# A fused attention and expert kernel: query parts loaded in three transfers in place of six, row maxima in one in place of four

## What is computed

```python
x = x + jnp.tanh(g_xattn[0]) * _L0_xattn_ref(_layernorm(x, axis=-1), ctx_1024, mask_BxSxS2_bf0, ...)
x = x + jnp.tanh(g_ffn[0]) * _L0_ffn_ref(_layernorm(x, axis=-1), ...)
x = x + jnp.tanh(g_xattn[1]) * _L1_xattn_ref(ctx_1024, ctx_1024, _layernorm(x, axis=-1), mask_BxS2_if0, ...)
x = x + jnp.tanh(g_ffn[1]) * _L1_ffn_ref(_layernorm(x, axis=-1), ...)
```

```python
q = heads(tgt @ Wq + bq) / jnp.sqrt(jnp.asarray(D_K, tgt.dtype))
k = heads(memory @ Wk + bk)
scores = jnp.einsum('bhqd,bhkd->bhqk', q, k)
scores = jnp.where(mask[:, None, :, :], NEG_INF, scores)
attn = jax.nn.softmax(scores, axis=-1)
```

## Time and profile before

| | |
|---|---|
| median of three runs | 831.93 us (830.88 to 833.39) |
| the profiled execution | 831.65 us, of which its span is 829.6 us |
| TensorE busy, matmuls | 594.7 us, 72% |
| VectorE busy | 487.7 us, 59% |
| ScalarE busy | 244.0 us, 29% |
| loads of query parts | 24 of 128 KB |
| loads of maxima | 16 of 12 KB |

### The profile page before, as it was taken

How to read it: one execution, slowest core, us unless ns; L and a number is a source line. 1 busy time by engine, 2 the same in 40 slices (tenths; PEclk the granted TensorE clock), 3 DMA queues, 4 the chain that set the end, 5 groups by cost and what they waited for, 6 DMA issues and landing times.

```text
span 829.6 us, 14684 instructions
## 1 busy us (share of the span) xinstructions
PE 594.7 (72%) x6038; PEld 418.9 (50%) x6038; DVE 487.7 (59%) x1173; ACT 244.0 (29%) x421; POOL 42.7 (5%) x52
## 2 busy tenths in 40 slices
PE   2256575968998699777777597988759998406563
PEld 1223122635376478653264486854428887405452
DVE  5736664544136635589446545687255475597765
ACT  0001352304555233204434232315335332201110
POOL 1700000000001100000002000000000000000000
PEclk9977696989999889799998897999979999757655
DMA  3390100210000268710000379300002684058440
GB/s 92 62 305 12 50 2 0 50 20 13 1 1 1 50 160 239 214 53 6 0 21 1 72 252 259 132 5 1 13 0 70 207 231 140 1 142 262 111 143 13
DMA packets 40354, 70.71 MB, mean 85 GB/s; under 512 B 9824, under 2 KB 26577, under 8 KB 40097
## 3 DMA queue, kind: packets, MB, share of 16 engines
q1 hardware_dynamic: 30796, 63.64, 27.6%
q10 hardware_dynamic: 9492, 6.14, 2.6%
HBM read 65.82 MB, written 3.95 MB: 84 GB/s over the span
## 4 chain that ended last, share of the span: by engine, by line
PE 49%; DVE 27%; DMA 9%; issue 6%; ACT 5%; SPq 2%; POOL 1%; POOLq 0%; DVEq 0%; ACTq 0%
PE DOWN L750 12%; PE UP L913 9%; PE RING L949 5%; PE RING L954 3%; DMA OHA<-scratch_positions 3%; DVE nmax L1240 3%; PE MISC L715 2%; PE RING L821 2%; DVE xn L1025 2%; PE MISC L724 2%; DMA OHA<-scratch_q_parts 2%; DVE OHA L1054 2%; DMA QAf<-scratch_q_parts 2%; DVE dots L1379 1%; DVE GV L1441 1%
## 5 line engine op out<-in xcount | busy, mean ns | idle before, releaser
L750 PEld LDWEIGHTS DOWN<-W,hT 128*128 128x128 f32 x1152 | 154.1, 197 | 21.9 <-issue 2.6
L750 PE MATMUL DOWN<-W,hT 128*128 128x128 f32 x1152 | 154.8, 280 | 0.2 <-ACT hT L661 0.2
L661 ACT ACTIVATE hT<-UP,b 128x512 f32<-128x512 f32 x144 | 98.3, 687 | 158.9 <-PE UP L913 158.5
L913 PE MATMUL UP<-xnTf,W 128*128 128x512 f16 x432 | 124.3, 403 | 3.4 <-ACT hT L661 3.0
L949 PE MATMUL RING<-TAB,OHA 128*128 128x32 f16 x2560 | 78.8, 180 | 53.6 <-DVE OHA L1054 32.4
L949 PEld LDWEIGHTS RING<-TAB,OHA 128*128 128x128 f16 x2560 | 74.4, 99 | 61.6 <-DVE OHA L1054 39.0
L688 ACT ACTIVATE GV<-RING 128x256 f32<-128x256 f32 x80 | 30.7, 383 | 149.9 <-PE RING L954 149.9
L1070 DVE SCALAR_TENSOR_TENSOR acc<-DOWN,W,acc 128x128 f32<-128x128 f32 x128 | 36.0, 344 | 59.6 <-PE DOWN L750 53.1
L1054 DVE TENSOR_SCALAR OHA<-OHA,cst 128x2048 f16<-128x2048 bf16 x80 | 59.5, 748 | 13.4 <-DMA OHA<-scratch_positions 12.7
L1240 DVE TENSOR_REDUCE nmax<-RING 128x3 f32<-128x462 f32 (+1 forms) x96 | 53.7, 585 | 19.2 <-PE RING L824 15.1
L913 PEld LDWEIGHTS UP<-xnTf,W 128*128 128x128 f16 x432 | 42.4, 103 | 35.2 <-issue 9.5
(11 more groups left out here) (321 smaller groups left out, 774.2 us busy)
## 6 DMA issues: line engine op xcount, KB each, us to landing
OHA<-scratch_positions SPq DMA_DIRECT2D x80, 512.0 KB, 5.6
OHA<-scratch_tail_positions SPq DMA_DIRECT2D x48, 160.0 KB, 4.9
OHA<-scratch_positions SPq DMA_DIRECT2D x16, 160.0 KB, 3.9
QAf<-scratch_q_parts SPq DMA_DIRECT2D x18, 128.0 KB
hT<-in_w ACTq DMA_DIRECT2D x3, 768.0 KB, 6.1
W<-in_w ACTq DMA_DIRECT2D x3, 768.0 KB
scratch_q_parts<-qs SPq DMA_DIRECT2D x4, 384.0 KB, 2.5
X<-in_x ACTq DMA_DIRECT2D x4, 256.0 KB, 4.9
```

Source lines behind the costliest of these rows:

```text
L661: act.activation(hT[:, i % HS, :], UP[:, i % 2, :], ACT.Silu, bias=b1[:, e, c:c + 1], scale=1.0 / W1SCALE).then_inc(h_ready, 1)
L750: last = pe.matmul(DOWN[:, n % 2, t * 128:(t + 1) * 128], hT[:, (k + c) % HS, t * 128:(t + 1) * 128], W2[:, e, c, :], start=(c == 0), stop ...
L913: last = pe.matmul(UP[:, i % 2, :], W1[:, pw, e, c * 128:(c + 1) * 128], xnTf[:, b % 2, px], start=(n == 0), stop=(n == 2))
```

## The change

The slots are renumbered, so that query parts 0, 1, 2 stand in slots 0 to 2, parts 0, 1 in slots 3 and 4, and part 0 in slot 5; the key parts are paired with them as before. The source rows of a run of slots are then one after the other in `scratch_q_parts`, and each of the three runs in `RUNS` is one load: 24, 16 and 8 partitions, with 16 KB on each. The maxima come back in one load of 3 partitions with 16 KB on each. The waits on `qa_in` and `qm_in` count three loads and one.

```diff
-SLOT_Q = (0, 0, 0, 1, 1, 2)
-SLOT_K = (0, 1, 2, 0, 1, 0)
+SLOT_Q = (0, 1, 2, 0, 1, 0)
+SLOT_K = (0, 0, 0, 1, 1, 2)
+RUNS = ((0, 3), (3, 2), (5, 1))
...
-                    for i, s in enumerate(SLOT_Q):
-                        sp.dma_start(QAs[b][i * DK:(i + 1) * DK], dq[b, s].rearrange("(d h) q -> d h q", d=DK)).then_inc(qa_in, 16)
+                    for at, n in RUNS:
+                        sp.dma_start(QAs[b][at * DK:(at + n) * DK].rearrange("p h q -> p (h q)"),
+                                     dq[b, 0:n].rearrange("s (d h) q -> (s d) (h q)", d=DK)).then_inc(qa_in, 16)
                     if b == 0:
-                        sp.wait_ge(qa_in, 16 * len(SLOT_Q))
+                        sp.wait_ge(qa_in, 16 * len(RUNS))
...
-                    for f in range(4):
-                        sp.dma_start(QAs[b][QR:QM, 4 * f:4 * f + 4].rearrange("s h q -> s (h q)"),
-                                     dm[b, :, 4 * f * NT:4 * (f + 1) * NT].rearrange("s e q -> s (e q)")).then_inc(qm_in, 16)
+                    sp.dma_start(QAs[b][QR:QM].rearrange("s h q -> s (h q)"),
+                                 dm[b].rearrange("s e q -> s (e q)")).then_inc(qm_in, 16)
...
-                act.wait_ge(qa_in, 16 * len(SLOT_Q))
+                act.wait_ge(qa_in, 16 * len(RUNS))
...
-                        pe.wait_ge(qa_in, 16 * len(SLOT_Q) * (b + 1))
+                        pe.wait_ge(qa_in, 16 * len(RUNS) * (b + 1))
...
-                        pe.wait_ge(qm_in, 16 * NT * (b + 1))
+                        pe.wait_ge(qm_in, 16 * (b + 1))
```

## The result

The change makes the kernel 0.8% faster: 825.37 us median (821.84 to 829.56, 20 runs) against 832.09 (828.48 to 835.09, 20 runs of the kernel before beside it), ratio 0.9915 with an interval of 0.990 to 0.993. That is 5.8 to 8.3 us where 14.2 were forecast, and the median lies outside the range of 812.5 to 823.6. The direction held; about half of the gain did not come. The profiled execution of after took 829.56 us (span 827.5), at the upper end of its runs, so a second trace of the same kernel (825.95 us) is read beside it.

A forecast was written before the change was run, and what follows sets the result against it. The prediction took the query loads, limited at their destination partitions, to hold up TensorE in batches 0 and 1. 6.2 + 1.5 + 5.8 + 1.0 - 0.3 = 14.2 us gave 817.7 us, range 812.5 to 823.6.

The forecast's parts named there:

- The set, 6.2 us earlier in batch 0: Query loads: three loads following one another take 6.3 us for 12.5, so the set lands 6.2 us earlier; bounds 5.3 to 8.2.
- What follows in batch 0: Issues behind the set move with it, WvT landing at about 50.4 for 56.6; VectorE's maxima hardly move; 6.2 us passed on.
- Clock in batch 0: After the shorter idling before the first table, part of 56.6 to 68.0 runs at the upper clock: 1.5 us, bounds 0 to 4.3.
- the prediction's last sign of being wrong: The upper clock level after the shorter waits is lost again at another place; no size given.
- Batch 1, the whole wait of 5.8: Before batch 1's score matmuls: the set lands at about 169.0, TensorE is free at 169.4, so 5.8 us of wait go.
- Clock in batch 1: Score stage of batch 1, entered without a pause, falls from 16.1 us towards 15.05: 1.0 us gained, bounds 0 and 1.0.
- Maxima: Maxima load of batch 0: one load for four lands 0.3 us later, bounds 0.2 earlier to 1.0 later; other batches not counted.
- Each row keeps its own pace: Rival, query loads: a 16 KB row takes 2.1 us whatever its neighbours do; set gains 4.2 us, kernel 821.8 us; chance 0.14.
- The load fell on no single engine: Rival, slower: one engine carries the whole 24-partition load, set 14.2 us later in batches 0 and 1, about 860 us; chance 0.04.
- the source gave more than 63 GB/s: Rival, no effect: the source gives 61 to 63 GB/s however rows are asked for, about 831 us; chance 0.05.
- WvT moved with the set: Rival, batch 0: something else holds WvT, so only TensorE's own wait of 2.7 us is won there; 823.4 us; chance 0.05.

The follow-up runs named there:

- query_only: The changed kernel's three query loads with the four maxima loads of the kernel before: 825.35 us, ratio 0.989 to the kernel before.
- short_first: The changed kernel with its three query loads issued in the opposite order, 8, 16, then 24 rows: 819.71 us, ratio 0.9851 to the kernel before.
- three16: The changed kernel with the query set cut into three loads of 16 neighbouring partitions, one maxima load kept: 821.11 us, ratio 0.9875 to the kernel before.
- wide: Against the changed kernel: three query loads of 16 rows to every second partition of 0-31 (twice) and 64-95, four maxima loads: 817.03 us, ratio 0.9805.
- maxima_only: The kernel before, keeping its six query loads, with the one maxima load of the change: 834.86 us against 834.28, ratio 1.0009.
- the battery: The changed kernel with fifteen groups of loads timed behind its last store: 24 neighbouring rows took 4.1 us, the set of 24+16+8 10.2.

## Where the prediction went wrong, and what held

- **The set, 6.2 us earlier in batch 0: 4.3.** This is the step that failed, in the words "On an engine they follow one another, so 6.3 us". The price of each load held (24 rows alone take 4.1 us from issue to landing, 8 rows 4.0). The sum did not: the loads do not use the same engines, so rows of the second start beside the first and slow it, and the set takes 10.2 us from its first issue in place of 8.2. The same three loads in the opposite order take 8.25 to 8.35. The prediction also took consecutive loads to reach different partitions, where partitions 32 apart share. The bounds failed with it: they ran from 5.3 to 8.2 and knew overlap only as a gain.
- **What follows in batch 0.** Right. WvT and the first table move with the set, 3.9 of 4.3 us. VectorE's first maximum stays (40.94; 41.08 in the earlier trace rows), and TensorE's wait for the set turns into one for VectorE, 4.24 us.
- **Clock in batch 0, 1.5: there, and lost again.** In the traces of after the way from the first table to the transposed scores shortens by 1.4 and 1.1 us (36.86 to 35.44 and 35.80) in spite of the later maxima. By the query store of batch 1 it is gone: the lead is 5.3 and 4.9 us at the transposed scores and 3.5 and 2.4 at that store (157.49 before, 153.98 and 155.06), with a granted clock of 0.77 between the two places in both traces, where it was 0.84 before. That is the prediction's last sign of being wrong. In query_only, with the same query loads, the clock is 0.87 there and nothing is lost, so the cause stays open. That less idling goes with a higher clock is borne out in part: over the 11.4 us from the first table the granted clock was 0.50 before, 0.68 and 0.64 in after, 0.85 in short_first, 1.00 in three16 and wide, but 0.69 in maxima_only too, with 7.2 us of idling ahead of it. A stretch like this differs by some 3 us between executions (33.98 us in maxima_only).
- **Batch 1, the whole wait of 5.8: 3.1.** The same step, and one more. The set took 14.8 us there before (160.41 to 175.22) and 11.75 after (156.86 to 168.61), so 2.73 us of wait stay. But three16, whose set takes the forecast 8.2 us in batch 0, takes 10.0 in batch 1: the prediction carried the gain of batch 0 over, and in batch 1 six key loads are issued right ahead of the set on the same queue (at 154.45 in after; the last of them is still moving when the set starts). What they cost was not tested apart. In short_first and wide no wait is left, as forecast.
- **Clock in batch 1, 1.0: 0.3.** The score stage takes 15.8 us (168.66 to 184.44) for 16.1, its first 4.1 us at a granted clock of 0.58 for 0.52. In three16, with 1.03 us of the wait left, they run at 1.00 and the stage takes 15.07 (161.00 to 176.07), the 15.05 of batch 3.
- **Maxima, 0.3 later: 0.7**, and in batch 2 0.2 to 0.45 more between issue and use (3.19 before, 3.64 and 3.40 after). Inside the bound of 1.0; mis-sized.
- **Sum.** 3.9 + 3.1 + 0.3 - 0.7 - 0.3 (batch 2) = 6.3 us, with the clock of batch 0 at nothing since it is lost again, beside the 6.7 measured (5.8 to 8.3).
- **The rivals.** "Each row keeps its own pace" had the size of the set right, 4.2 us, by a mechanism that the battery refutes: 24 rows alone would have taken 6.1 us, spread rows 4.0, and the order would not have mattered. Its 821.8 lies just under the lowest of the runs, since it too counted 1.5 us of clock and took the wait of batch 1 for 4.2 us shorter. The load fell on no single engine (twelve rows start at once), the source gave more than 63 GB/s, and WvT moved with the set.

## What to carry to other kernels

A queue of loads costs about the sum of its loads where each uses the same engines (three pairs of 16 rows took 6.1 to 6.5 us where 6.1 was due). Behind a load that leaves engines free the next one starts early, and that can be a loss: 24 then 16 rows took 8.6 us, 16 then 24 only 6.6. So try the order of unequal loads, or give all the same number of rows. For rows of 16 KB to few partitions, choose the partitions: three loads of 16 rows took 8.3 us to neighbours, 7.85 to every third of 0-47, and 5.8 to every second of 0-31 and 64-95. When a range is made, let overlap be a loss too, and a gain found in one place smaller in another.

## What the runs showed of the hardware

- Four neighbouring partitions together take some 30 GB/s: three loads of 16 rows (four groups of four each) against one, 4.36 us more for 524 KB (8.27 less 3.91), 120 GB/s over four groups. Partitions 32 apart share it (four loads of 8 rows: 6.9 us against 5.55). The Trainium skill's page on SBUF, in the section named above, has 27.2 GB/s for such a port; the rows give somewhat more.
- The order of three loads is worth 2 us of 10 (10.2 against 8.25), with nothing else changed.
- The 24 rows of a load start twelve at a time, as on twelve engines with two rows each; a load queued behind it starts its first rows beside the second twelve (the windows above).
- A load to every second to eighth partition takes SyncE longer to issue, 0.5 to 0.8 us in place of 0.3 to 0.4.
- The same work takes up to 3 us more or less from one execution to the next: from the transposed scores of batch 2 to the layer normalisation near 446 us, 64.9 us before (385.44 to 450.35), 67.45 and 64.7 in the two traces of after, at the granted clocks shown above.
